# A graph network on one core: TensorE's one-hot sums ahead of, instead of behind, the group's other products in two edge stages

## What is computed

```python
# first layer (L0): one message per edge, summed by destination
edge_feat = concatenate([V[src], V[dst], one_hot(rel, 8)])
h = relu(edge_feat @ W1 + b1)
out = segment_sum(h @ W2 + b2, dst)
# third layer (L2): plain normalised sums of gathered rows
out = segment_sum(dis[row] * dis[col] * (x @ W.T)[row], col) + b
# computed in the same stage for the fourth layer: a two-layer net of the edge features, twice
wk = relu(edge_attr_64 @ k_w1 + k_b1) @ k_w2 + k_b2
wv = relu(edge_attr_64 @ v_w1 + v_b1) @ v_w2 + v_b2
```

## Time and profile before

| | |
|---|---|
| median of three runs | 4083.49 us |
| profiled execution | 4080.55 us, of which the span from its first to its last instruction is 4078.8 us |
| mean granted TensorE clock | 0.753 of full speed |
| PE busy | 2660.5 us (65%) in 13300 instructions |
| VectorE busy | 2327.1 us (57%) |
| GpSimd busy | 2074.5 us (51%) |
| ScalarE busy | 870.6 us (21%) |
| products of stage 1 (L458 and L459, PE) | 236.8 and 230.0 us, 832 instructions each |
| one-hot sums of stage 1 (L445, PE) | 173.0 us, 832 instructions |
| H, W and S of stage 3 (L1577, L1569, L1585, PE) | 127.6, 205.7 and 138.0 us |

### The profile page before, as it was taken

The page is one execution under the profiler, slowest core; times in us unless marked ns, Lnnn a source line. Parts: engine busy times, 40 slices in busy tenths (PEclk is TensorE's granted clock), DMA queues, the critical chain, the costliest instruction groups (busy, mean ns, idle before and its releaser), DMA issues. The chain is left out here.

```text
span 4078.8 us, 50401 instructions
## 1 busy us (share of the span) xinstructions
PE 2660.5 (65%) x13300; PEld 2199.8 (54%) x13300; DVE 2327.1 (57%) x5139; ACT 870.6 (21%) x2423; POOL 2074.5 (51%) x2126
## 2 busy tenths in 40 slices
PE   2577767613444445256667655888887878887886
PEld 2466667612433344235545544766776766666772
DVE  2344444515777787734444532666665666666676
ACT  0000000114455554001111100222221222222222
POOL 3666656144666662266666506555555555455530
PEclk7665665655565655578998967999998889899995
DMA  2233333144555451034444416766666666666640
GB/s 60 60 69 68 70 68 69 30 128 96 126 123 127 123 126 45 22 100 126 137 130 133 135 69 155 168 152 156 153 160 149 152 148 161 150 157 154 152 117 8
DMA packets 340429, 462.27 MB, mean 113 GB/s; under 512 B 171147, under 2 KB 203020, under 8 KB 339990
## 3 DMA queue, kind: packets, MB, share of 16 engines
q1 hardware_dynamic: 252048, 254.61, 26.8%
q0 software_dynamic: 73216, 150.93, 14.7%
q10 hardware_dynamic: 14976, 54.53, 3.6%
HBM read 394.55 MB, written 65.27 MB: 113 GB/s over the span
## 5 line engine op out<-in xcount | busy, mean ns | idle before, releaser
L1925 PE MATMUL psum<-ckv,z 128*128 128x256 f32 x4160 | 1057.4, 402 | 66.1 <-issue 63.3
L1925 PEld LDWEIGHTS psum<-ckv,z 128*128 128x128 f32 x4160 | 809.4, 202 | 210.6 <-issue 101.8
L1818 POOL DMA_INDIRECT acc<-QW,dst_i x416 | 393.1, 945 | 575.7 <-DVE vw L1987 458.8
L987 POOL DMA_INDIRECT ga<-T,src_i x416 | 432.1, 1039 | 357.8 <-PE psum L1100 132.9
L277 POOL DMA_INDIRECT ga<-TA,src_i x416 | 414.9, 997 | 247.6 <-DVE pre L484 131.6
L277 POOL DMA_INDIRECT ga<-T,src_i x416 | 400.0, 962 | 238.9 <-issue 112.2
L1826 POOL DMA_INDIRECT ga<-XX,src_i x416 | 400.0, 961 | 153.3 <-issue 126.5
L1972 DVE TENSOR_TENSOR z<-psum,shb 128x2560 f32<-128x2560 f32 x104 | 293.4, 2821 | 155.1 <-DMA win<-T1W 88.6
L458 PE MATMUL psum<-wre,re 128*128 128x68 f32 x832 | 236.8, 382 | 216.5 <-DMA win<-TB 138.9
L2016 DVE TENSOR_TENSOR acc<-acc,psum 128x256 f32 x416 | 175.5, 422 | 278.2 <-DMA win<-T1W 197.8
L458 PEld LDWEIGHTS psum<-wre,re 128*128 128x128 f32 x832 | 195.5, 289 | 242.0 <-issue 167.6
(11 more groups left out here) (348 smaller groups left out, 4296.0 us busy)
## 6 DMA issues: line engine op xcount, KB each, us to landing
shb<-in_ea SPq DMA_DIRECT2D x104, 640.0 KB
WKV<-wkvo ACTq DMA_DIRECT2D x104, 512.0 KB
shb<-in_ea SPq DMA_DIRECT2D x104, 512.0 KB
wkv<-WKV SPq DMA_DIRECT2D x104, 512.0 KB
dl<-DL SPq DMA_DIRECT2D x208, 128.0 KB
win<-TB SPq DMA_DIRECT2D x416, 32.0 KB
ga<-T,src_i POOLq DMA_INDIRECT x832
ef<-in_ea SPq DMA_DIRECT2D x104, 128.0 KB
```

Source lines behind the costliest of these rows:

```text
L987: pool.indirect_dma_start(ga[:, ring(g) + t, :], None, T1, bass.IndirectOffsetOnAxis(ap=src_i[:, g * GT + t:g * GT + t + 1], axis=0)).then ...
L1818: pool.indirect_dma_start(qg[:, (g % QR) * GT + t, :], None, QW, bass.IndirectOffsetOnAxis(ap=dst_i[:, g * GT + t:g * GT + t + 1], axis=0) ...
L1925: last = pe.matmul(kv_of(k)[:, t, :], z[:, k % 2, j, t * 128:(t + 1) * 128], ckv[:, j, :], start=(j == 0), stop=(j == NZ - 1))
```

## The change

In stage 1 the sums of group g - 2 are issued at the head of TensorE's `body` of group g, ahead of its waits for `oneT`, `re` and the windows, and not behind its products. In stage 3 `networks` of group g - 1 is issued behind the one-hot sums of group g, and not ahead of them. No instruction is added or removed, and no buffer changes. What is issued after the loops stays as it was.

```diff
@@ -448,6 +448,8 @@
                 def body(i, k):
                     g = i * UG + k
+                    if back(i, k, 2):
+                        sums(*back(i, k, 2))
                     pe.wait_ge(e0_oT, g + 1)
                     pe.wait_ge(e0_rel, g + 1)
                     pe.wait_ge(e0_w[k], i * 64 + 64)
...
                     last.then_inc(e0_P, 1)
-                    if back(i, k, 2):
-                        sums(*back(i, k, 2))
                 each_group(pe, body)
@@ -1575,8 +1575,6 @@
                     pe.matmul(bank[2 + k % 2][:], w1kv[:], ef[:, k % ER, :], start=True, stop=True).then_inc(e2_H, 1)
-                    if before(i, k):
-                        networks(*before(i, k))
                     pe.wait_ge(e2_one, g + 1)
                     pe.wait_ge(e2_g[k], i * 64 + 64)
                     wait(pe, e2_acc, (g - 1) * GT)
...
                     last.then_inc(e2_S, 1)
+                    if before(i, k):
+                        networks(*before(i, k))
                 pe.wait_ge(e2_pad, 1)
```

## The result

The changed kernel takes 4113.24 us in the median of five runs (4105.04 to 4119.15), beside 4083.49 us before: a ratio of 1.0072, 95% interval [1.0055, 1.0090], slower by 30 us. The forecast was 4192 us, slower by 108. The direction held, the size did not.

A forecast was written before the change was run, and what follows sets the result against it. Stage 1 was taken as paced by SyncE's issue, stage 3 by two-group cycles with TensorE completions held during GpSimd's gathers. 4080.55 + 0 + 100 + 9 = 4189.6, plus 2.9 for the median: 4192 us, range 4090 to 4300.

The forecast's parts named there:

- Stage 1, costed at nothing: Stage 1: moving the sums ahead of TensorE's waits costs 0, since SyncE's issue of window loads sets the pace.
- bounds of -37 and +50 us: Stage 1: half of a 73 us gain in window waits and half of a 100 us loss from late messages.
- The loop of stage 3: Stage 3: `one`, S, W, bias, next `one` closes on every group instead of every second, 4.78 us a group.
- The tail, +9 us: Stage 3 after the last gather: seven groups left, each 4.78 instead of 3.48 us, 7 x 1.30 = +9 us.
- While GpSimd gathers, +100 us: Stage 3 during gathers: between longer pauses (+132 to +179 us) and a stop after each group (+72), taken as +100.
- the 1.60 us in the pause of 4.81 or 5.83: Stage 3: held TensorE completions come out 1.60 us after GpSimd stops, first term of a 4.81 or 5.83 us pause.
- I expect both mixed: Stage 3: two regimes, second S unmade when GpSimd stops (+132 to +179 us) or made but held back (+72); +100 taken.
- nothing moves: Rival, stage 3: W comes out in the pause that exists anyway, only the stage's end shows; 4092 us, chance 0.12.
- every W is held until GpSimd stops: Rival, stage 3: each group pays a whole pause, 9.5 us a group, +336, about 4425 us; chance 0.10.
- the sums hide in stage 1: Rival, stage 1: TensorE paces it and the sums fill its window waits, -73, about 4119 us; chance 0.08.
- Faster: Rival, stage 3: S signalled one W sooner, 47 pauses of 2.0 us all but vanish, -89 us, 3994 us; chance 0.10.
- The clock falls: Rival, stage 3: more idling keeps TensorE at 1.2 GHz, 7.7 us a group, about 4275 us; chance 0.10.

The follow-up runs named there:

- run with the wait for the bias: Kernel before, plus one TensorE wait in stage 3: S(g) waits until the bias of g - 1 is done, old order kept; 4175.62 us, 1.0202.
- the changed kernel with the later bias: Changed kernel with VectorE's bias in stage 3 two groups behind instead of one; 4077.42 us, 0.9980.

## Why the prediction was right in direction and wrong in size

*Stage 1, costed at nothing: right.* The run with that half alone is at 0.9998. That SyncE's issue is the cover fits SyncE's missing waits, but was not tested by itself. Its bounds of -37 and +50 us were not needed.

*The loop of stage 3: right, also in its price.* 4.78 us a group were worked out, 4.88 measured, with gathers over and with gathers left out; cutting it at the bias takes the whole loss away.

*The tail, +9 us: a term of the right kind, mis-sized.* It is +16: 8 groups instead of 7 are left behind the last gather (3.5 us), each takes 1.40 us more instead of 1.30 (11 us), and one of them 1.6 us more again, as its W took 3.44 us instead of 1.89 behind a wait.

*While GpSimd gathers, +100 us: this step failed.* It measured +19. The sum had it right that S, on which GpSimd waits, is not made when GpSimd stops: in 37 of the 44 pauses above 1 us (from 1790 us on) it ends behind the burst, where before it ended 1.1 to 5.0 us ahead of the burst's end in all 45. The term that failed is the 1.60 us in the pause of 4.81 or 5.83: it lets the W that opens this S out only after GpSimd has stopped, by the reading that completions held back "come out together some 1.60 us after it stops". Measured, the bias behind this W started 1.0 to 4.0 us ahead of the burst's end in 39 of the 44 pauses, and 0.3 to 2.2 us behind it only in the five of 4.5 to 6.5 us. The rest of the chain is as forecast: in one pause the bias starts 1.22 us ahead of the end; with 1.96 us to S, 2.06 of S and 0.27 to the restart that makes 3.07 us, the length of that pause. In 24 of the pauses S's own signal is late as well, by 0.3 to 2.7 us. That the pauses of the changed kernel are nearly as long as those before is thus in part a coincidence: the chain from W to S now fills time in which S's signal was held before.

In the changed kernel W starts right behind S and mostly ends in one of the first six gathers of a burst. In the first four it passes on time there; in the fifth and sixth it is held some 2 us and mostly comes out while GpSimd goes on. The reading was taken from the kernel before alone, where W, S, H and W queue up behind one another and do come out together, behind the burst. The run with the wait for the bias shows the reading's own price, where it holds half of the time: +80 us. That mixture stood in the prediction ("I expect both mixed"), but between the wrong two ends: the case in which the pause stays as it was had been left to the rival *nothing moves*, at 0.12 and 4092 us, and the truth lies 21 us above that rival and 79 below the forecast.

*The rivals.* That every W is held until GpSimd stops (4425 us) is out, 36 of the 64 W's of the table's first row passed without being late. That the sums hide in stage 1 is out. *Faster*, because S is signalled sooner: its condition was that `one` is ready when H ends, and it is not: 124.9 us of waiting are put down to `one`, 125.1 before, and TensorE's idle time ahead of S is 230.9 us by all releasers, 195.4 before. *The clock falls*: the granted clock of the stretch is 0.87 against 0.88, so the extra idling hardly moved it, and the rule of the Trainium skill that was weighed there ("TensorE: Matmul & The Clock Gate", "Why this matters for your kernels") did not decide this change. W's busy time did grow from 205.7 to 228.2 us, by blocks of 2.4 to 3.6 us instead of 1.89 (26, where before 9 took 2.3 us or more). These alone cost nothing that shows: the changed kernel with the later bias has more of them (W busy 238.9 us) and its stretch takes 614.6 us.

*The signs that were named.* The one for wrong, 47 pauses that stay at 2 us, came nearly: 46, of which 25 near 2 us. The stretch grew to 635 us and not to some 700 to 750. The groups of 4.8 us behind the last gather came, at 4.87.

*What stays open.* Why a W held back in the sixth gather comes out amid the burst in the changed kernel (11 of 14), but as the burst ends or after it in the kernel with the extra wait (21 of 23), and why the kernel before never lets one out early, not even one that ends in the third or fourth gather; why W's come out 50.5 us apart when there are no pauses; what in GpSimd's gathers holds TensorE's completions was narrowed down (not the stores; the gathers, more so the denser they come), not found. Whether a pitch between 1.25 and 1.39 us would do was not tried.

The best version run is the changed kernel with the later bias, 0.9980 [0.9960, 0.9999] of the kernel before: it undoes the loss, and a gain is hardly to be told from none.

## What to carry to other kernels

Moving work of an in-order engine ahead of other work closes or opens loops through the engines that wait for it; write the loop out with its durations, as it will be paid in full where nothing hides it (147 us here) and hardly at all where another engine's pace does (19 us). An idle gap of the pacing engine need not be recoverable: seven of the kernels here, with different orders, stores and gaps, all took 615 to 623 us for the gathers of stage 3. A pause that keeps its length need not keep its cause: look at what ends it. A pattern of late signals read from one order of work should not be carried over to another order, for the order sets when in the burst a signal is raised.

## What the runs showed of the hardware

TensorE's completions reach other engines late while GpSimd issues indirect gathers; without gathers none was (from 1775 us on in the two runs that leave them out). In the changed kernel, in its stage-3 half alone and in the kernel with the wait for the bias, those that ended in the first four gathers behind a pause of 1.2 us or more (410 that can be told, from 1790 us on) came out 0.01 us behind their ends, but for four that were 0.4 to 1.1 us late. In the kernel before that does not hold: 8 of 8 W's that ended in the third or fourth gather were held 6 to 9 us, and W's in general 0.5 to 9 us. When GpSimd gathered for 557 us without a pause the lateness settled at 24 to 74 us, with one W out every 50.5 us. In the traces before and after the change VectorE's and ScalarE's completions were never late (0.013 us at most). Left to itself GpSimd did 416 gathers in 557 us, 1.34 us each, against 1.48 with its pauses.
